# Routed experts' weights split into high and low parts once, stored to DRAM, and read through a ring of four slots

## What is computed

```python
x_flat = x.reshape(N, C)                                  # 4096 x 512
shared_out = einsum('nh,dh->nd', silu(x_flat @ sw1.T) * (x_flat @ sw3.T), sw2)   # width 1024
s = sigmoid(x_flat @ router_w.T + t_bias_flat)            # 8 experts
_, topk_idx = top_k(s + router_bias, 2)
H = gelu(einsum('nd,ehd->enh', x_flat, rw1))              # width 256, per expert
O = einsum('enh,edh->end', H, rw2)
routed_out = einsum('end,ne->nd', O, combine)             # only the 2 chosen have weight
out = (shared_out + routed_out) / 3
```

## Time and profile before

| | |
|---|---|
| median of 3 runs | 2918.16 us (2914.73, 2918.16, 2922.99) |
| span of the profiled execution, first to last instruction | 2914.5 us |
| its own time as a run | not given apart; the fastest run shown is 2914.73 us |
| TensorE's matmuls busy | 2574.8 us, 88% |
| VectorE / ScalarE / GpSimd busy | 1479.1 / 1200.6 / 724.8 us |
| moved by DMA | 328.58 MB |

### The profile page before, as it was taken

One profiled execution on the slowest core, in us unless ns is written; L12 is line 12 of the kernel. 1 busy time (PEld: TensorE's weight loads), 2 busy tenths in 40 slices (PEclk: granted clock), 3 DMA queues, 4 the chain that ended last, 5 costly groups with the idle time before them and its releaser, 6 DMA issues. The chain is left out here.

```text
span 2914.5 us, 41950 instructions
## 1 busy us (share of the span) xinstructions
PE 2574.8 (88%) x12487; PEld 2061.8 (71%) x12487; DVE 1479.1 (51%) x1826; ACT 1200.6 (41%) x1773; POOL 724.8 (25%) x604
## 2 busy tenths in 40 slices
PE   6999999977787568888888886699997999999999
PEld 1788888866666456666666664599996888888876
DVE  4311111146666577777777774477664233333346
ACT  3111111146676455555555552466664222222223
POOL 0222222021222146555555554000000111111100
PEclk9999999989899889999999998799998999999999
DMA  6222222034634253335333531566664111111125
GB/s 246 33 63 51 51 51 43 14 120 121 195 109 130 88 172 121 123 122 177 118 122 120 176 121 65 205 231 224 232 237 163 37 29 33 33 29 29 29 76 169
DMA packets 136778, 328.58 MB, mean 113 GB/s; under 512 B 41762, under 2 KB 44258, under 8 KB 129056
## 3 DMA queue, kind: packets, MB, share of 16 engines
q1 hardware_dynamic: 113744, 258.70, 27.1%
q0 software_dynamic: 22992, 69.37, 8.1%
HBM read 425.67 MB, written 77.76 MB: 173 GB/s over the span
## 5 line engine op out<-in xcount | busy, mean ns | idle before, releaser
L1083 DVE TENSOR_TENSOR s_w_lo<-s_w_raw,s_w_hi 128x1024 fp32r<-128x1024 f32 x256 | 354.1, 1421 | 3.0 <-ACT s_w_hi L1041 3.0
L1041 ACT ACTIVATE s_w_hi<-s_w_raw 128x1024 fp32r<-128x1024 f32 x256 | 256.6, 1052 | 103.8 <-PE s_z_ps L88 72.3
L395 DVE TENSOR_TENSOR s_h<-s_sg,s_up 128x512 f32<-128x512 f32 x64 | 43.9, 687 | 395.7 <-ACT s_sg L290 395.6
L86 PE MATMUL s_g<-wx_hi,s_x_hi 128*128 128x512 f32 x512 | 206.7, 404 | 6.5 <-DVE s_x_lo L1604 4.0
L88 PE MATMUL s_g<-wx_hi,s_x_lo 128*128 128x512 f32 x512 | 201.8, 394 | 0.0
L87 PE MATMUL s_g<-wx_lo,s_x_hi 128*128 128x512 f32 x512 | 201.1, 393 | 0.0
L607 POOL DMA_INDIRECT s_x<-in_x_rows,s_idx x72 | 92.4, 1284 | 405.5 <-DMA s_idx<-mid_slot_token 387.0
L1338 DVE TENSOR_TENSOR s_w_lo<-s_w_raw,s_w_hi 128x1024 fp32r<-128x1024 f32 x128 | 150.9, 1221 | 68.1 <-ACT s_w_hi L1290 66.4
L290 ACT ACTIVATE s_sg<-s_gate 128x512 f32<-128x512 f32 x64 | 38.3, 599 | 291.2 <-PE s_up L88 291.2
L86 PE MATMUL s_z_ps<-s_w_hi,s_ht_hi 128*128 128x512 f32 x256 | 110.6, 432 | 50.8 <-DVE s_ht_lo L1099 47.4
L1505 POOL DMA_INDIRECT s_y<-mid_hash_out,s_rec x32 | 31.5, 985 | 488.2 <-DMA s_rec<-mid_rec 488.2
(11 more groups left out here) (305 smaller groups left out, 7296.8 us busy)
## 6 DMA issues: line engine op xcount, KB each, us to landing
s_w_raw<-in_rw SPq DMA_DIRECT2D x144, 512.0 KB
s_w_raw<-in_w SPq DMA_DIRECT2D x32, 2048.0 KB
s_w_raw<-in_w SPq DMA_DIRECT2D x64, 1024.0 KB
s_w_raw<-in_w1h SPq DMA_DIRECT2D x16, 2048.0 KB, 8.2
s_w_raw<-in_w2h SPq DMA_DIRECT2D x16, 2048.0 KB, 7.7
mid_routed<-s_o_sb SPq DMA_DIRECT2D x72, 256.0 KB, 3.1
s_b<-in_b SPq DMA_DIRECT2D x32, 512.0 KB
s_x_grp<-in_xt_groups POOLq DMA_DIRECT2D x8, 1024.0 KB, 5.7
```

The source lines that it names most:

```text
L86: pe.matmul(out, a_hi, w_hi, start=first, stop=False, skip_group_check=True)
L1041: act.activation(hi[:, c], raw[:, c], ACT.Copy).then_inc(S[name + "_hi"], 1)
L1083: dve.tensor_tensor(lo[:, c], raw[:, c], hi[:, c], ALU.subtract).then_inc(S[name + "_lo"], 1)
```

## The change

The weights of the routed experts are split once instead of once per tile, in the shared stage: SyncE loads each expert's weights in two parts of 512 KB (w1, w2), ScalarE and VectorE make high and low parts in chunks 3 and 7 of a group (one expert per group), and SyncE stores them to a new tensor in DRAM, `mid_rw`, 1 MB per part. The loading of x and the storing of the output move from SyncE to ScalarE's queue. GpSimd no longer loads the records back from DRAM tile by tile but takes them from SBUF.

In the routed stage SyncE loads both parts, high and low together, 1 MB, from `mid_rw` into one of four slots of a buffer `w`. The slot comes from a table that VectorE writes at the end of the shared stage (the number of the expert in the order of use, modulo 4), kept in the buffer `order`. `new` now compares a tile with the one before it. `load_w` loads three values instead of two (expert, new, slot) and waits for TensorE's matmuls of four tiles before. TensorE loads the slot into a register twice per tile (`find_weights`) and addresses its weights by it. ScalarE's and VectorE's splits are gone from this stage. The lags on SyncE are 0, 0, 1, 4, 4 instead of 0, 2, 3, 4, 7.

```diff
@@ stage_shared, SyncE
-            def load_x(g):
...
-            def store_o(g):
...
+            def raw_part(e, j):
+                sp.dma_start(w_raw[:, j % 2], ins["rw"][e, :, j * HS:(j + 1) * HS]).then_inc(S[f"part_in{j % 2}"], 16)
+
+            def store_part(e, j):
+                sp.dma_start(d["rw"][e, :, j], part[j % 2]).then_inc(S[f"part_out{j % 2}"], 16)
+
+            def parts(e, last=False):
+
+                for j in range(NPART):
+                    sp.wait_ge(S["part_lo"], e * NPART + j + 1)
+                    store_part(e, j)
...
@@ stage_shared, GpSimd
-                    pool.dma_start(rec_tile[:, k], d["rec"][i2 * 2 + k]).then_inc(S["rec_in"], 16)
...
@@ stage_shared, ScalarE
+            def part_hi(g, j):
...
+                act.wait_ge(S[f"part_in{j % 2}"], turn * 16 + 16)
+                wait_for(act, S[f"part_out{j % 2}"], turn * 16)
+                act.activation(part[j % 2][:, 0].bitcast(FP32R), w_raw[:, j % 2], ACT.Copy).then_inc(S["part_hi"], 1)
+
+            def load_x(g):
+                act.wait_ge(S["xt_lo"], g)
+                act.dma_start(x_raw, ins["xt_groups"][g]).then_inc(S["xt_in"], 16)
+
             def chunks(g):
...
+                    if c == 0 and not (isinstance(g, int) and g == G - 1):
+                        load_x(g + 1)
...
+                    if c in PART_CHUNKS:
+                        part_hi(g, PART_CHUNKS.index(c))
...
+                    act.dma_start(d["shared"][g * TG + m], o_sb[:, m % 2]).then_inc(S[f"o_out{m % 2}"], 16)
@@ stage_shared, VectorE
-            op(dve.tensor_tensor(new[:, 2:RT], te[:, 2:RT], te[:, 0:RT - 2], ALU.not_equal))
+            op(dve.tensor_tensor(new[:, 1:RT], te[:, 1:RT], te[:, 0:RT - 1], ALU.not_equal))
...
+            op(dve.tensor_tensor_scan(used, te[0:1], new[0:1], 0.0, ALU.mult, ALU.add))
+            op(dve.tensor_copy(slot, used))
+            op(dve.tensor_scalar(slot, slot, NW2 - 1, None, ALU.bitwise_and))
@@ stage_routed
-        w_raw = sb("w_raw", [P, 2, W1 + W2])
-        w_hi = sb("w_hi", [P, 2, W1 + W2], FP32R)
-        w_lo = sb("w_lo", [P, 2, W1 + W2], FP32R)
+        w = sb("w", [P, NW2, 2, 2, HS], FP32R)
...
+        def slot(eng, i):
+            return eng.value_load(slots[0:1, bass.ds(i, 1)], min_val=0, max_val=NW2 - 1)
@@ stage_routed, SyncE
-            def load_w(name, c):
+            def load_w(layer, used):
                 def stage(i, n, turn):
                     expert = sp.value_load(route[0:1, 0, bass.ds(i, 1)], min_val=0, max_val=ER - 1)
                     new = sp.value_load(route[0:1, 1, bass.ds(i, 1)], min_val=0, max_val=1)
-                    wait_apart(sp, S[name + "_lo"], i - 1)
-                    sp.dma_start(w_raw[:, n % 2, c], ins["rw"][expert, :, c],
-                                 cond=new > 0).then_inc(S[f"{name}_in{n % 2}"], 16)
+                    s = slot(sp, i)
+                    wait_apart(sp, S[used], i - NW2 + 1)
+                    sp.dma_start(w[:, bass.ds(s, 1), layer].bitcast(FP32),
+                                 d["rw"][bass.ds(expert, 1), :, layer].rearrange("o p s n -> p o s n"),
+                                 cond=new > 0).then_inc(S[f"w{layer + 1}_in{n}"], 16)
                 return stage
...
-            software_pipeline(sp, RT, [(0, load_idx), (2, load_w("w1", slice(0, W1))),
-                                       (3, load_w("w2", slice(W1, W1 + W2))), (4, load_wo), (7, store)], NI)
+            software_pipeline(sp, RT, [(0, load_idx), (0, load_w(0, "mm1")), (1, load_w(1, "mm2")), (4, load_wo),
+                                       (4, store)], NI)
@@ stage_routed, ScalarE and VectorE: w1_hi, w2_hi, w1_lo, w2_lo are gone
-            software_pipeline(act, RT, [(2, gelu), (1, x_hi_), (0, w1_hi), (3, o_copy), (2, h_hi), (1, w2_hi),
-                                        (3, wo_hi)], NI)
+            software_pipeline(act, RT, [(2, gelu), (1, x_hi_), (3, o_copy), (2, h_hi), (3, wo_hi)], NI)
...
-            software_pipeline(dve, RT, [(1, x_lo_), (0, w1_lo), (2, h_lo), (1, w2_lo), (3, wo_lo)], 2)
+            software_pipeline(dve, RT, [(1, x_lo_), (2, h_lo), (3, wo_lo)], 2)
@@ stage_routed, TensorE
+            def find_weights(name):
+                def stage(i, n, turn):
+                    now[name] = slot(pe, i)
+                return stage
+
+            def weights(name, layer, part, c):
+                return w[:, bass.ds(now[name], 1), layer, part, c].rearrange("p o n -> p (o n)")
...
-            software_pipeline(pe, RT, [(2, up), (1, turn_x), (3, down), (2, turn_h)], NI)
+            software_pipeline(pe, RT, [(2, find_weights("up")), (2, up), (1, turn_x), (3, find_weights("down")), (3, down),
+                                       (2, turn_h)], NI)
```

More of the change, by code:

```diff
@@ L30 @@
 EPS = 1e-9
+NW2 = 4
 DVE_BIG = 3.0e38
@@ L215, in _ @@
                 units(u2)
-            def load_x(g):
[L218 to L221, removed]
-            def store_o(g):
[L224 to L228, removed]
-            units(NU // 2 - 1)
-            software_pipeline(sp, G, [(0, but_first(load_x)), (1, store_o)])
-            sp.wait_ge(S["o_out"], 16 * NB)
+            sp.wait_ge(S["logits_t"], G - 1)
+            sp.dma_start(x_raw, ins["xt_groups"][0]).then_inc(S["xt_in"], 16)
+            units(NU // 2 - 1)
+            def raw_part(e, j):
[6 more added lines that the diff above has]
+                    store_part(e, j)
+                    if j + 2 < NPART:
+                        raw_part(e, j + 2)
+                    elif not last:
+                        raw_part(e + 1, j + 2 - NPART)
+            sp.wait_ge(S["w_lo"], NU)
+            raw_part(0, 0)
+            raw_part(0, 1)
+            with sp.Fori(0, ER - 1) as e:
+                parts(e)
+            parts(ER - 1, last=True)
+            for n in range(2):
+                sp.wait_ge(S[f"part_out{n}"], 16 * ER * NPART // 2)
         @block.gpsimd
@@ L308, in _ @@
             software_pipeline(act, G, [(1, chunks), (0, but_first(x_hi)), (1, o_out)])
+            for n in range(2):
+                act.wait_ge(S[f"o_out{n}"], 16 * NB // 2)
         @block.vector
@@ L388, in x_lo, with part_lo, late_parts @@
                 dve.tensor_tensor(xt_lo[:], x_raw, xt_hi[:], ALU.subtract).then_inc(S["xt_lo"], 1)
+            def part_lo(g, j):
+                dve.wait_ge(S["part_hi"], g * NPART + j + 1)
+                dve.tensor_tensor(part[j % 2][:, 1].bitcast(FP32R), w_raw[:, j % 2], part[j % 2][:, 0].bitcast(FP32R),
+                                  ALU.subtract).then_inc(S["part_lo"], 1)
+            def late_parts(g):
+                for j in range(len(PART_CHUNKS), NPART):
+                    part_lo(g, j)
             def chunks(g):
@@ L399, in chunks @@
                                           ALU.subtract).then_inc(S["h_lo"], 1)
+                    if c in PART_CHUNKS:
+                        part_lo(g, PART_CHUNKS.index(c))
             x_lo(0)
```

106 lines of the change are left out of this document (48 added, 58 removed).

## The result

The changed kernel takes **3016.76 us** (median of 4 runs, 3014.64 to 3017.7) where the kernel before takes 2916.93 (median of 4, 2914.73 to 2922.99): a ratio of **1.034**, 95% interval 1.0323 to 1.0354. The span of its profiled execution is 3014.8 us, 100.3 more than before.

The account below looks back on a forecast made before the run. SyncE's instruction queue was taken to bound the routed stage. Terms 101 + 10 + 1.5 - 4 - 4 = +104 us gave 2914.5 + 104 = 3018.5 for the profiled execution, forecast median 3022 us (+3.6%), range 2990 to 3090.

Parts of the forecast that it names:

- The bound: Routed stage: SyncE's instruction queue sets the pace, 5.32 us per step before the change.
- The sign that was named: Routed stage, if right: SyncE's index loads 6.5 to 7.1 us apart, with hardly a wait.
- The price of a value: SyncE, routed stage: loading one value into a register costs 0.457 + 3 x 0.045 = 0.59 us.
- The price of an expert load: SyncE, routed stage: each load gains 0.59 + 0.12 + 0.03 = 0.74 us, bounds 0.59 and 0.91; 137 loads, +101 us.
- No wait on SyncE: Routed stage: tile out some 26 us after its index load, store at 33 us, so SyncE's new waits cost nothing.
- The small terms: SyncE, routed stage: four more expert loads +10 us, three more stores +1.5, fewer loads carried out -4.
- The drain behind the last index load: End of routed stage: 18.3 us instead of 22.6 behind the last index load, so -4 us.
- TensorE: Routed stage: added values and ISA rows cost nothing; upper bound 2.4 us, 6.0 us per tile, below SyncE's 6.8.
- The rival in which TensorE becomes the bound: Routed stage: TensorE's step above 6.8 us, at 7.6 us per tile +172 us, 3090 us; chance 0.14.
- The splits: Routed stage: removed splits, 152 us and 177 us over 72 tiles, lie beside SyncE's step; no gain credited.
- The shared stage: 16 added splits, loads and stores hide under TensorE's 522.71 us; stage stays at 524 us within 3.
- The rule of the Trainium skill that was weighed: SyncE's issue time, routed stage: by this rule the 104 us would be 0, leaving the removed splits' gain; prediction disagreed.

Follow-up runs that it names:

- the dummy: Kernel before, with a third, unused value read on SyncE (the new-flag again) in each conditional expert load: 2986.21 us, ratio 1.0224.
- the short queue: Changed kernel, SyncE reading two values per tile instead of six; second expert load, square matrix, store and TensorE's second slot read moved: 2874.22 us, ratio 0.9845.
- the kernel before with one read: Kernel before, with expert and new-flag read once per tile for both layers' loads, both at lag 3: 2879.19 us, ratio 0.9855.
- the narrow splits: Kernel before, with expert-weight splits of 16 columns instead of 1024 in the loop's tiles: 2922.52 us, ratio 1.0009.
- the store moved to ScalarE: Short queue with TensorE's slots read behind matmuls, plus the routed tiles' store issued by ScalarE behind the copy: 2879.18 us, ratio 0.9861.
- the three kernels with the short queue and the store on SyncE: Short queue (2874.22 us); it with TensorE's slots read behind matmuls (2869.01); the latter with TensorE's weights from a fixed slot (2857.51).

## Why the prediction was right, and where it was off

**The bound** was named rightly. Adding reads to SyncE (+66 us), and taking them away (-41 and -91) move the time, and relieving TensorE of its register work (-1) or ScalarE and VectorE of the splits (+3) doesn't. The sign that was named, index loads 6.5 to 7.1 us apart, came out at its lower edge: 6.46 in the mean, 6.38 at the median.

**The price of a value**, 0.59 us, measured 0.61 for the slot in the loop of the changed kernel (from its start to the next record, 1.21 per tile for two) and 0.56 for the dummy.

**The price of an expert load** was too high: 0.74 was put down, and the step grew by 6.46 - 5.32 = 1.14 us, 0.57 per load, just under the lower bound of 0.59. The address arithmetic, an estimate of 0.12, measured 0.085 with its step, and the register instruction, put at 0.03, is in the 0.61 above. What failed is the silent assumption that everything else stays: the first value read of a step, of which the kernel before has one behind each index load too, became 0.19 us per tile shorter. That gives 0.61 + 0.085 - 0.095 = 0.60, still 0.03 more than the step shows. In the sum, 137 x 0.57 = 78 us instead of 101.

**No wait on SyncE** held in the loop, where there is none to speak of, and failed in the head. The step that failed is "a tile is out 26 us after its index load, its store comes at 33": it took the steady step for all tiles and did not follow `wo_hi`, which stands on ScalarE ahead of the copies and waits for a load that SyncE issues one or two steps later. Behind the store at lag 4 this cost 10 us. So the two errors, 23 us too much and 10 too little, offset each other in part: the forecast is nearer than its terms.

**The small terms.** The last index load moved by 99.9 us, where 101 + 10 + 1.5 - 4 = 108.5 was put down. With the terms as measured, 78 for the loads, 10 for the wait of the head, and the small ones as they were (+10, +1.5, -4), it is 95.5; some 4 us of it have no name. Of the 144 expert loads 14 are carried out, where 26 were. The drain behind the last index load was put at 18.3 us, and the last copy on ScalarE shows it:

```profile
1090.85 0.60 ACT L682 ACTIVATE s_o_sb<-s_o 128x512 f32<-128x512 f32 x1 [2.31 <-PE s_o L89]
```

1090.85 + 0.60 - 1073.7 = 17.8, so 4.8 us were gained there. They are not in the end time: from the last index load to the end of the span it is 1940.7 us before and 1941.1 after. Over the thirteen traces of this study this stretch lies between 1935.0 and 1947.3, so whether the gain was lost in the next stage or in this scatter stays open.

**TensorE** put at nothing: right, by the run that relieves it. The rival in which TensorE becomes the bound had one condition come true: its granted clock fell. From 700 to 900 it was 0.94 in the kernel before at 76% busy, and in the changed kernel:

```profile
700.00:900.00 200.00, 138.69 (x740) 114.35 (x738) 34.33 (x62) 56.82 (x123) 29.15 (x31) 0.87 0.41 132
```

0.87 at 69% busy, a mean of 2.4 and 1.2 GHz with about a quarter of the stretch at the lower level. Even so TensorE waited 91 us of 350 for the gather. With the short queue it is 0.98 at 86%. The busy share doesn't settle it, though: the kernel before with one read, where TensorE stands idle for several us at a time behind new experts, has 0.91 at 84%:

```profile
700.00:900.00 200.00, 167.25 (x985) 142.02 (x986) 140.02 (x167) 149.59 (x248) 45.50 (x41) 0.91 0.54 166
```

The Trainium skill's page "TensorE: Matmul & The Clock Gate", part "The HAM clock gate (the "warmup" mystery)", has the clock fall after idle time; 0.94 at 24% idle and 0.87 at 31% agree with it in direction. That all of the stage is at the lower clock, which the rival wanted, did not come.

**The splits** credited with nothing: right, and shown by the narrow splits. **The shared stage** at nothing: right, 524 us within 1.

The rule of the Trainium skill that was weighed, on "DMA: Bandwidth & Descriptors", section "Issuing engines are not separate DMA queues", that a sequencer's time to start a DMA "is usually small relative to the DMA itself", doesn't bound what such a DMA costs its queue here. The issue itself is short, 0.09 us where the load is skipped, but the reads that decide on it are the dear part: one more per load cost 66 us, and sharing them between two loads gave 41.

## What to carry to other kernels

A transfer that is usually skipped still costs its whole preparation on the queue that issues it: price a conditional DMA by the values read for it and their range arithmetic, not by its bytes, and read values once for all DMAs that use them. Before work is moved off an engine, ask which queue the step really waits for; here ScalarE and VectorE lost 253 us of work, net, for nothing, and two values per tile instead of six, with some places moved, turned a kernel 3.4% slower into one 1.6% faster. Where a startup load is consumed by an in-order engine, follow it through the first steps by hand, since the steady step does not describe them.

## What the runs showed of the hardware

A value read doesn't always take the same time. In the changed kernel, in the step from 803.4 (lines of SyncE in three stretches within it), the expert's read behind the index load took 0.50 us, the new-flag's and the slot's, further back, 0.28 and 0.27:

```profile
L628 SPq TENSOR_LOAD <-route x1: 500/500/500, 803.6 to 803.6; - x1
```

```profile
L629 SPq TENSOR_LOAD <-route x2: 275/278/281, 804.5 to 807.1; - x2
```

From the thirteenth step on this first read took 0.66 us in the mean in the kernel before (up to 1.13), 0.54 with the third read and 0.47 in the changed kernel, and the others 0.27 or less. This is most of why an added read of 0.56 us lengthened the step by 0.49 only.

That it stands right behind the index load's issue isn't the reason. With the short queue the expert's number is read in the same place and takes 0.27 us at the median. With the store moved to ScalarE it is the second read that is long (667 to 929 and 667 to 936):

```profile
L630 SPq TENSOR_LOAD <-route x59: 45/269/700, 669.9 to 925.4; - x59
```

```profile
L619 SPq TENSOR_LOAD <-order x60: 264/481/1042, 668.1 to 932.6; - x60
```

What the long reads share is the time since the last store of a tile (`mid_routed`) was issued, by SyncE or by ScalarE. In the loops of the thirteen traces 452 of SyncE's reads start 0.7 to 1.3 us after it, and 96% of them take over 0.35 us; of the 2016 that start more than 2 us after it, 1.4% do. In the three kernels with the short queue and the store on SyncE no read starts in that window. The kernel with the store on ScalarE differs from the one ahead of it in the store alone, and there the long read appears; but no run was made to test this, the reason isn't known, and the count doesn't tell why the reads in the window took 0.72 us in the kernel before and 0.53 in the changed one.
